# First attention of a post-norm decoder layer: the stream of row maxima shifted by four steps

## What is computed

```python
q, k, v = qkv[0], qkv[1], qkv[2]                 # B=4, H=16 heads, N=1024 tokens, D=16
q = q * cos + _rotate_half(q) * sin
k = k * cos + _rotate_half(k) * sin
attn = jnp.einsum('bhqd,bhkd->bhqk', q, k) * SCALE
diff = jnp.where(diff > 0, 0.0, pos[None, :] - pos[:, None])
attn = attn + (diff[None] * slopes[:, None, None] * MAX_BIAS)[None]
w = jax.nn.softmax(attn, axis=-1)
out = jnp.einsum('bhqk,bhkd->bhqd', w, v)
...
x = _layernorm(x + out_projection)               # then cross attention, then 8 experts, top 2
disp = jnp.zeros((E, CAP, Cx), x.dtype).at[ids_f, pos_c].add(xr * keep[:, None])
```

## Time and profile before

| | |
|---|---|
| median of three runs | 1902.18 us (1900.19 to 1906.13) |
| the profiled execution | 1905.45 us, span 1903.6 us |
| busy in the span | TensorE 1637.1 us, VectorE 1302.4, ScalarE 993.9, GpSimd 403.4 |
| reductions of maxima, line 638 | 512, 602.3 us, 1220 ns each |
| exponentials, line 622 | 1024, 547.7 us, 596 ns each |
| granted TensorE clock | mean 0.915 of 2.4 GHz |

### The profile page before, as it was taken

How to read it: one execution, slowest core, us unless ns; L and a number is a source line. 1 busy time by engine, 2 the same in 40 slices (tenths; PEclk the granted TensorE clock), 3 DMA queues, 4 the chain that set the end, 5 groups by cost and what they waited for, 6 DMA issues and landing times. The chain is left out here.

```text
span 1903.6 us, 36270 instructions
## 1 busy us (share of the span) xinstructions
PE 1637.1 (86%) x14816; PEld 1066.9 (56%) x14816; DVE 1302.4 (68%) x2288; ACT 993.9 (52%) x1692; POOL 403.4 (21%) x268
## 2 busy tenths in 40 slices
PE   7848999999999999999585699867993999999970
PEld 6724444444444444443274555545763888888870
DVE  6777888888888888884185637752333677777736
ACT  5323777777777777777434157853441333333310
POOL 6540000000000000000134200001552344444430
PEclk9956999999999999999788659988996999999995
DMA  7878454444544445410365858314213233333225
GB/s 254 194 181 236 59 67 66 68 68 64 69 63 70 64 66 67 64 29 9 120 198 184 116 75 135 79 48 137 90 40 109 67 92 92 92 92 92 37 32 178
DMA packets 131421, 183.98 MB, mean 97 GB/s; under 512 B 30918, under 2 KB 95572, under 8 KB 130200
## 3 DMA queue, kind: packets, MB, share of 16 engines
q1 hardware_dynamic: 117816, 159.60, 39.8%
q0 software_dynamic: 13440, 22.07, 5.4%
HBM read 114.99 MB, written 69.99 MB: 97 GB/s over the span
## 5 line engine op out<-in xcount | busy, mean ns | idle before, releaser
L638 DVE TENSOR_REDUCE att_row_max<-att_ring 128x2 f32<-128x1024 f32 x512 | 602.3, 1220 | 108.4 <-PE att_ring L704 56.9
L622 ACT ACTIVATE att_w_exp<-att_s_ps 128x512 f32<-128x512 f32 x1024 | 547.7, 596 | 232.3 <-PE att_s_ps L747 156.8
L774 PE MATMUL att_a_ps<-att_w_exp,att_v_group 128*32 128x512 f32 x2048 | 273.6, 606 | 0.2 <-ACT att_w_exp L622 0.2
L733 PE MATMUL att_s_ps<-att_q_stack,att_k_stack 62*128 62x512 f32 x640 | 181.5, 480 | 0.0
L733 PEld LDWEIGHTS att_s_ps<-att_q_stack,att_k_stack 62*128 62x128 f32 x640 | 84.4, 184 | 124.0 <-ACT att_w_exp L622 112.7
L2166 ACT ACTIVATE ex_hid<-ex_h_ps,ex_b 128x512 f32<-128x512 f32 x128 | 87.1, 685 | 118.0 <-DVE ex_h_lo L2221 64.8
L2122 POOL DMA_INDIRECT x_scr<-ex_y,ex_home x64 | 106.7, 1668 | 182.3 <-DVE ex_y L2211 167.6
L560 POOL COPY att_eyes<-keep_slope_eye 128x384 bf16<-128x384 bf16 x16 | 8.1, 507 | 641.5 <-PE att_s_ps L747 632.2
L2221 DVE TENSOR_TENSOR ex_h_lo<-ex_hid,ex_h_hi 128x512 fp32r<-128x512 f32 x128 | 138.8, 1085 | 4.4
L704 PE MATMUL att_ring<-att_k_stack,att_q_stack 60*128 60x512 f32 x640 | 131.3, 450 | 6.2 <-DVE att_att L665 3.2
L747 PE MATMUL att_s_ps<-att_eyes,keep_past_bf 64*128 64x64 bf16 x3840 | 133.1, 193 | 0.0
(11 more groups left out here) (291 smaller groups left out, 3550.1 us busy)
## 6 DMA issues: line engine op xcount, KB each, us to landing
first_w_raw<-ew SPq DMA_DIRECT2D x16, 1024.0 KB, 7.5
att_k_stack<-qk_scr SPq DMA_DIRECT2D x120, 128.0 KB
cr_q_stack<-q_scr SPq DMA_DIRECT2D x48, 256.0 KB, 9.4
keep_k_stack<-qk_scr SPq DMA_DIRECT2D x72, 128.0 KB
rows_scr<-att_zeros POOLq DMA_DIRECT2D x8, 1040.0 KB, 22.6
ex_rows<-rows_scr SPq DMA_DIRECT2D x16, 520.0 KB, 4.9
att_q_stack<-qk_scr SPq DMA_DIRECT2D x60, 128.0 KB
qk_scr<-qkv_t_hi SPq DMA_DIRECT2D x7, 1024.0 KB, 4.3
```

Source lines behind the costliest of these rows:

```text
L622: nc.scalar.activation(w_exp[(STEPS * g.n + st) % SETS][h][:, :], s_ps[v % BANKS][:, :], ACT.Exp).then_inc(exp_done, 1)
L638: nc.vector.tensor_reduce(out, ring[place.slot][:, :, :], AX.X, ALU.max).then_inc(ring_free, 1)
L733: ins = nc.tensor.matmul(s_ps[v % BANKS][:, :], ks[g.buf][rows, c, j, kt * P:(kt + 1) * P], qs[g.buf][rows, j, c * CH:(c + 1) * CH], start ...
L774: ins = nc.tensor.matmul(a_ps[32 * h:32 * h + 32, :], vg[g.buf][:, kt, h * VW:h * VW + 32], w_exp[(STEPS * g.n + st) % SETS][h][:, :], sta ...
```

## The change

The stream of maxima is moved back by four steps against the scores. 24 units instead of 32 stand in front of window 0; window g holds the last 8 units of its own group (steps 0 to 3) and the first 24 of the next (steps 4 to 15), so window 15 has 8 units. Top 0 of group 0 is taken behind unit 17 instead of 19. In the windows top 1 is transposed at step 5 instead of 1 and top 0 of the next group at step 13 instead of 9; steps 8 and 0 still wait for them. TensorE's wait for the next group's stack moves from step 0 to 4. The accumulators stay at steps 2 and 10. SP's order follows: the att store of half 1 now stands ahead of top 1, the stack loads still behind top 1, and the att store of half 0 ahead of top 0. The eight stores of zeros leave the place before window 0; GpSimd issues one in each of windows 1 to 8, behind its copy of v. The core of the diff:

```diff
-TOP0_AT = 19
+TOP0_AT = 17
+LATE = 4
+AHEAD = UNITS - 2 * LATE
+TOP1_STEP, TOP0_STEP, ACC1_STEP, ACC0_STEP = LATE + 1, LATE + 9, 2, 10
+def max_units(n, st):
+    if st < LATE:
+        return [(n, AHEAD + 2 * st + i) for i in range(2)]
+    return [(n + 1, 2 * (st - LATE) + i) for i in range(2) if n < NG - 1]
...
             def window(g, with_max, has_last):
+                if has_last:
+                    store_att(sp, g.plus(-1), 1, PLACES[g.n - 1, "acc", 1])
                 move_top(sp, g, 1, PLACES[g.n, "top", 1])
...
                     load_stacks(sp, io, new, qs[new.buf], ks[new.buf], stack_in[new.buf])
-                if has_last:
-                    store_att(sp, g.plus(-1), 1, PLACES[g.n, "acc", 1])
+                store_att(sp, g, 0, PLACES[g.n, "acc", 0])
                 if with_max:
-                    move_top(sp, g.plus(1), 0, PLACES[g.n, "top", 0])
-                store_att(sp, g, 0, PLACES[g.n, "acc", 0])
+                    move_top(sp, g.plus(1), 0, PLACES[g.n + 1, "top", 0])
...
-            for a in range(8):
-                pool.dma_start(rows[a], zeros[:, :]).then_inc(zeroed, 16)
...
                     take_v(g.plus(1))
+                if 0 < g.n <= 8:
+                    pool.dma_start(rows[g.n - 1], zeros[:, :]).then_inc(zeroed, 16)
...
-            for u in range(UNITS):
-                max_pair(g0, u, PLACES[None, "max", u])
+            for u in range(AHEAD):
+                max_pair(g0, u, PLACES[0, "max", u])
...
                 for st in range(STEPS):
+                    if st == LATE and with_max:
+                        n = g.plus(1)
+                        pe.wait_ge(eye_ready, g.n + 2)
+                        pe.wait_ge(stack_in[n.buf], 16 * STACK_DMAS * (n.lap + 1))
...
-                    if with_max:
-                        for i in range(2):
-                            max_pair(n, 2 * st + i, PLACES[g.n, "max", 2 * st + i])
+                    for m, u in max_units(g.n, st):
+                        max_pair(Group.of(m), u, PLACES[m, "max", u])
```

More of the change, by code:

```diff
@@ L414, with ring_order @@
 RING_SLOTS = 2
-TOP0_AT = 19
-def ring_order(first, with_max):
+TOP0_AT = 17
[6 more added lines that the diff above has]
+    return [(n + 1, 2 * (st - LATE) + i) for i in range(2) if n < NG - 1]
+def ring_order(n):
     order = []
     for st in range(STEPS):
-        if st == 1:
-            order.append(("top", 1))
-        if st == 2 and not first:
-            order.append(("acc", 1))
-        if st == 9 and with_max:
-            order.append(("top", 0))
-        if st == 10:
-            order.append(("acc", 0))
-        order += [("max", 2 * st + i) for i in range(2) if with_max]
+        if st == ACC1_STEP and n:
+            order.append((n - 1, "acc", 1))
+        if st == TOP1_STEP:
+            order.append((n, "top", 1))
+        if st == ACC0_STEP:
+            order.append((n, "acc", 0))
+        if st == TOP0_STEP and n < NG - 1:
+            order.append((n + 1, "top", 0))
+        order += [(m, "max", u) for m, u in max_units(n, st)]
     return order
@@ L442, in ring_places @@
 def ring_places():
-    order = [(None, "max", u) for u in range(TOP0_AT + 1)] + [(None, "top", 0)]
-    order += [(None, "max", u) for u in range(TOP0_AT + 1, UNITS)]
+    order = [(0, "max", u) for u in range(TOP0_AT + 1)] + [(0, "top", 0)]
+    order += [(0, "max", u) for u in range(TOP0_AT + 1, AHEAD)]
     for n in range(NG):
-        order += [(n, what, i) for what, i in ring_order(n == 0, n < NG - 1)]
-    order.append((NG - 1, "acc", "end"))
+        order += ring_order(n)
+    order.append((NG - 1, "acc", 1))
     return {key: Place(at) for at, key in enumerate(order)}
@@ L823, in _ @@
                 values(last, st)
-            transpose_acc(last, 1, PLACES[last.n, "acc", "end"])
+            transpose_acc(last, 1, PLACES[last.n, "acc", 1])
 EPS = 1e-5
```

55 lines of the change are left out of this document (25 added, 30 removed).

## The result

| | before | after |
|---|---|---|
| median | 1904.16 us (1897.31 to 1916.76, 6 runs) | 1964.22 us (1957.44 to 1974.71, 6 runs) |
| profiled execution, its span | 1905.45, 1903.6 | 1964.30, 1962.5 |
| mean granted clock of TensorE | 0.915 | 0.901 |

The ratio is 1.0325, with a 95% interval of 1.029 to 1.0359: the change costs 60 us. In the source of after the lines of the attention are 10 or 11 higher: scores L743, bias L757, values L784, maxima L714 and L649, SP's store and readback of top L521 and L525.

What follows compares the result with a forecast made beforehand. It took the loop of scores, exponentials and values through three score banks to pace the windows. Start -7.8, stall +38.5, clock +12 and zeros +4 sum to +46.7 us; against the median of 1902.18 that is 1949 us, range 1915 to 1985.

Steps and rivals of the forecast that it cites:

- the signs that it named: In the trace: first score at 153 to 157, windows 1 to 13 of 50 to 52 us, readback 5 to 8 behind store.
- What paces a window: In the windows: scores, exponentials and values through three score banks set the pace, so maxima moved to any window cost 0.
- Start, -7.8: Before window 0: 8 fewer units bring the first score from 163.0 to 155.2, -7.8 us.
- Stall at the openings, +38.5 with +4 for the zeros: At 14 window openings: top 0's readback 2.75 us late on average, +38.5 us; zero blocks in windows 1 to 8, +4.
- the overtaking that the rival needed: In the windows: top 0's late store overtakes the stack loads, no window waits, 1894 us; chance 0.09.
- Clock, +12: Behind the opening waits: TensorE at half clock, a third of 3 us lost in 12 windows, +12 us.
- the ends 3 and 9: Half clock behind a wait: 3 us as in 1021 to 1024, or 9.16 us as in the first window (+42).
- Stages behind: Behind the attention: nothing is edited there, so no term, 0 us.
- absorption of half of the stall: Behind the opening waits: first steps run below 3.0 us and win back half, about 1925 us; chance 0.13.
- the clock did rise again: Answers a rival in the windows: clock stays down behind each stall, +42 instead of +12, about 1979 us; chance 0.12.

Runs made afterwards that it cites:

- e1: Changed kernel with the stack loads of windows 1 to 13 split: side 0 at the window's opening, side 1 behind top 1; 1898.66 us, ratio 0.9984.
- e7: Changed kernel with stack loads split in windows 1 to 13, and group 1's side 1 behind top 0's readback before window 0; 1892.25 us, ratio 0.993.
- e4: Changed kernel with the eight zero stores put back in front of window 0; 1978.34 us, ratio 1.0391.
- e8: Kernel before with only the zero stores moved, one block in each of windows 1 to 8; 1900.94 us, ratio 0.9967.
- e10: Changed kernel with each zero store held until 8 of its window's 64 score tiles are done; 1966.76 us, ratio 1.0312.
- e2: Kernel before with only the stack loads held until 30 of the window's 64 score tiles are done; 1989.56 us, ratio 1.045.
- e9: Kernel before with the stack loads split: side 0 behind top 1, side 1 behind top 0's readback (steps 11 to 15); 1907.96 us, ratio 1.0017.

## Why the prediction was right, and where it was off

The forecast was 1949 us with a range of 1915 to 1985; 1964 is within, 15 us above the forecast. Of the signs that it named, the windows came out longer than foreseen (50.8 to 54.9 us against 50 to 52) and the readback later behind its store (6.5 to 9.6 us against 5 to 8). Step by step:

- *What paces a window*: right. Maxima in other windows cost nothing: window 14 takes 47.38 us, and e1 and e7 have the change's whole rearrangement at 47.4 per window.
- *Start, -7.8*: -8.2. The first score was foreseen for 155.2 and came at 152.84, or 154.8 with the stage ahead of it as long as before. e4 and e8 show that both parts were needed: fewer units alone gain nothing there (41.39 us from the first maxima matmul to the first score, before 41.33), spread zeros alone 3.5 us, both together 8.2.
- *Stall at the openings, +38.5 with +4 for the zeros*: 40.4 measured. The split is not quite as foreseen: some 33.5 us for the queue, less than foreseen since window 1 opened without a wait (an "issue" idle time of 2.34 us had come first, in window 0) and windows 3, 6, 9, 13 and 14 with 0.3 to 1.6 us, and 7 for the zero blocks in four windows, which e10 takes out. That the sum came out within 2.1 us is partly luck. The Trainium skill ("DMA: Bandwidth & Descriptors", section "Queues, rings and completion order") says that completion is not first in, first out per issuing engine. Read as the prediction read it, a small store may overtake, and the forecast would be 1894 us; the 9.57 us of window 1, against 1.40 in e1, speak against it. But the same paragraph says ahead of this that the semaphore increment lands only after every earlier write from that DMA engine, across its queues, and its example of a completion out of order is a transfer on one DMA engine behind one on sixteen: so it does not promise the overtaking that the rival needed. The trace agrees with the rule on the increment: what SP waits for is the increment, and it came 6.5 to 9.6 us behind the store with loads ahead of it, 1.39 us without.
- *Clock, +12*: the term that was mis-sized; 24 measured. The price per us was right, a third (the 24 are what is left of the windows, no row's own number). The duration was not: I took 3 us of half clock for 12 windows, 36 us, and it was 72: over 6 us behind one wait, as the row of window 4 shows, and more behind the "issue" idle times. The nearest rows, 1021 to 1024 and the first window's 9.16 us, were the ends 3 and 9, and I took the lower end whole; the middle would have come to 24. The Trainium skill ("TensorE: Matmul & The Clock Gate", part 1, "HAM oscillation") describes half clock returning at every turn of a loop that waits for DMA: the trace agrees, all eight openings of after that waited 2.3 us or more had half clock behind them.
- *Not foreseen, +9*: the "issue" idle times. No row of before showed one on the bias matmuls; e2 shows that they come with late loads, e9 that late steps alone don't bring them, and the packets' records that TensorE's instructions were late.
- *Stages behind*: 0 foreseen, -4.3 measured, on unchanged code. In the other kernels' profiles the same stages take 1019.7 to 1036.8 us (before 1023.6, after 1019.4), so no run ties this term to the change. It is luck that it and the 2 us ahead brought the result nearer to the forecast: the change's own terms are +65 against +46.7.
- The rivals: no overtaking; no absorption of half of the stall, as the windows grew by more than their waits (that each us of wait costs one is not shown, and e10 took 7 us out without a gain in time); and the clock did rise again, though later than I took it.

The terms by their measured sizes are -8.2 + 40.4 + 24 + 9 = +65; with 2 us less ahead and 4.3 less behind, 58.9, the difference of the spans.

## What to carry to other kernels

A transfer's deadline must be counted through everything that is ahead of it on its queue: a bulk load that is harmless 8 steps ahead of a small move keeps holding that move when both shift, while the deadline stays. When a pipeline is shifted, split the bulk loads so that the queue is empty when the small move comes; half a stack at each of two quiet places turned +60 us into -13 (moving them whole the other way was not tried). And price a wait of 2 us or more on a busy TensorE at its length plus the slow stretch behind it, here another half of it again.

## What was not expected of the hardware

- A full stack (26 transfers) ahead of a small store in the queue holds it for 9.57 us in window 1 of after and 15.75 in e2; half a stack, issued 19 us ahead, hardly: 1.40 us there, and in e1's windows with loads at most 3.40.
- A zero block of 1.06 MB issued within 0.7 us of a small readback lengthens its flight from 2.8 to between 4.1 and 4.7 us, although the block takes only 2.5 us of all engines (an estimate from the earlier trace rows); one issued 1.84 us ahead did not (2.94). With the whole pile of eight it is 6.49 (e4).
- In after, all of TensorE's idle times of 1.8 us and more in the windows had half clock at or behind them. Of the shorter ones, waits of 0.99, 1.39 and 1.55 us (windows 3, 6 and 9) had none; but one of 1.56 us, 0.9 us behind a stop of 1.82, had, an "issue" idle time of 1.35 us in window 5 had (3.4 us of it), and in e4 a wait of 2.93 us had none: in these traces the length of the idle time alone does not decide it.
- TensorE stood still for 0.6 to 2.3 us at a time in after with no semaphore to wait for, only in windows in which a whole stack was landing late, at the same places of its program in several kernels, until 1.3 to 2.0 us behind the end of a 16 KB packet of its own instructions.
